# Last pass of a two-convolution residual block: the loads from the fourth input on move from SyncE's queue to ScalarE's

## What is computed

```python
def block(x, w1, b1, gamma1, beta1, w2, b2, gamma2, beta2):
    identity = x
    out = conv3x3(x, quantize_weight(w1, 8), b1)
    out = relu(batchnorm(out, gamma1, beta1))      # statistics over all images
    out = conv3x3(out, quantize_weight(w2, 8), b2)
    out = batchnorm(out, gamma2, beta2)            # statistics over all images
    return relu(out + identity)

return x + block(_gn(x), w1, b1, gamma1, beta1, w2, b2, gamma2, beta2)
```

## Time and profile before

| | |
|---|---|
| timed runs (3), median | 525.36 us (524.45 to 526.71) |
| profiled execution, its own time | 525.32 us |
| span of the profiled execution | 523.5 us |
| PE busy in the span | 489.3 us (93%) |
| DVE busy | 453.3 us (87%) |
| ScalarE (ACT) busy | 367.6 us (70%) |
| DMA queue 1 (SyncE's): share of the 16 engines | 45.9% of the span |
| DMA queue 10 (ScalarE's): share | 0.2% |

### The profile page before, as it was taken

The page is one execution under the profiler, slowest core; times in us unless marked ns, Lnnn a source line. Parts: engine busy times, 40 slices in busy tenths (PEclk is TensorE's granted clock), DMA queues, the critical chain, the costliest instruction groups (busy, mean ns, idle before and its releaser), DMA issues.

```text
span 523.5 us, 23701 instructions
## 1 busy us (share of the span) xinstructions
PE 489.3 (93%) x10987; PEld 401.3 (77%) x10987; DVE 453.3 (87%) x648; ACT 367.6 (70%) x408; POOL 86.8 (17%) x155
## 2 busy tenths in 40 slices
PE   4999999999999999999999999999998898978982
PEld 2888777778999787899888889889887466557541
DVE  7999989999999966998887898878796989998894
ACT  4799899999899964766656555566631899686471
POOL 2027356666651200000000000000001000000000
PEclk9999999999999999999999999999998999989997
DMA  8934785543333000001344300000047899999997
GB/s 289 351 131 132 256 274 171 193 134 134 131 136 130 9 10 7 3 4 62 129 173 152 128 3 4 3 4 4 3 160 270 327 387 416 424 397 422 396 427 320
DMA packets 23242, 92.99 MB, mean 178 GB/s; under 512 B 8168, under 2 KB 9576, under 8 KB 19048
## 3 DMA queue, kind: packets, MB, share of 16 engines
q1 hardware_dynamic: 22960, 91.19, 45.9%
q10 hardware_dynamic: 184, 0.30, 0.2%
HBM read 58.27 MB, written 32.28 MB: 173 GB/s over the span
## 4 chain that ended last, share of the span: by engine, by line
PE 85%; DVE 8%; issue 2%; ACT 2%; DMA 1%; DVEq 0%; SPq 0%; ACTq 0%
PE conv_ps L1423 71%; PE conv_ps L1568 5%; PE conv_ps L1591 4%; PE conv_ps L1545 2%; DVE slots L1318 2%; DVE slots L1296 2%; DVE slots L1302 2%; PE conv_ps L1386 1%; DMA slots<-in_x_dram 1%; PE conv_ps L1553 1%; DVE bn_tup L1105 1%; DVE split L1325 0%; ACT split L822 0%; ACT conv_ps L796 0%; DVE xa L1318 0%
## 5 line engine op out<-in xcount | busy, mean ns | idle before, releaser
L1423 PE MATMUL conv_ps<-split,wmat 64*64 64x385 f16 (+3 forms) x9216 | 380.3, 324 | 0.7 <-ACT split L627 0.7
L1423 PEld LDWEIGHTS conv_ps<-split,wmat 64*64 64x64 bf16 x9216 | 326.2, 107 | 50.9 <-issue 1.4
L661 ACT ACTIVATE slots<-conv_ps,par,evac_scale 128x784 f32<-128x784 f32 x124 | 123.7, 998 | 94.6 <-PE conv_ps L1423 92.8
L1105 DVE BATCH_NORM_STATS2 bn_tup<-slots 128x6 f32<-128x392 f32 x164 | 80.8, 555 | 12.8 <-ACT slots L661 12.8
L992 DVE BATCH_NORM_STATS2 small<-slots 128x6 f32<-128x448 f32 x112 | 61.7, 612 | 0.8 <-DMA slots<-in_x_dram 0.8
L1070 DVE TENSOR_TENSOR split<-slots,split 128x3136 f16<-128x3136 f32 (+4 forms) x36 | 57.2, 1607 | 3.6 <-ACT split L627 0.8
L1072 DVE SCALAR_TENSOR_TENSOR split<-slots,split 128x3248 f16<-128x3248 f32 (+3 forms) x18 | 53.6, 2979 | 2.3
L1048 DVE TENSOR_SCALAR slots<-slots,bn_w 128x3248 f32<-128x3248 f32 (+3 forms) x18 | 30.4, 1687 | 19.6 <-ACT split L617 19.1
L617 ACT ACTIVATE split<-slots,bn_w 128x3248 f16<-128x3248 f32 x14 | 43.1, 3082 | 0.0
L669 ACT ACTIVATE xa<-conv_ps,par,evac_scale 128x784 bf16<-128x784 f32 x40 | 39.8, 997 | 0.0
L617 ACT ACTIVATE split<-slots,gn_b_all,gn_s_all 128x3136 f16<-128x3136 f32 x12 | 35.9, 2993 | 0.0
(11 more groups left out here) (159 smaller groups left out, 414.9 us busy)
## 6 DMA issues: line engine op xcount, KB each, us to landing
slots<-in_x_dram SPq DMA_DIRECT2D x13, 1568.0 KB, 11.5
slots<-in_x_dram SPq DMA_DIRECT2D x51, 392.0 KB, 5.2
out_dram<-slots SPq DMA_DIRECT2D x12, 784.0 KB, 8.4
out_dram<-slots SPq DMA_DIRECT2D x6, 1568.0 KB, 7.7
y_spill<-slots SPq DMA_DIRECT2D x3, 1624.0 KB, 6.2
slots<-y_spill SPq DMA_DIRECT2D x3, 1624.0 KB, 7.3
xa<-in_x_dram SPq DMA_DIRECT2D x2, 1568.0 KB, 11.0
split<-in_x_dram SPq DMA_DIRECT2D x2, 1568.0 KB, 10.2
```

The lines of the kernel that those rows point to most:

```text
L661: nc.scalar.activation(dst, src, ACT.Identity, bias=bias, scale=scale, accum_out=total).then_inc(evacuated[ph], 1)
L1105: ins = nc.vector.bn_stats(bn_tup[:, 2 * (n - first) + s, :], rows[s])
L1423: return nc.tensor.matmul(bank[:, r0:r1, w0:w1], lhs, rows[:, top + r0:top + r1, w0 + kx - 1:w1 + kx - 1], start=n == 0 and part is hi_all ...
```

## The change

All loads from input 4 on, and the reload of kept sums for input 15, are taken off SyncE's list and put into ScalarE's, each with its wait, at a chosen place. Their order among themselves is the same. The stores stay on SyncE's list in the same order, and so do the loads of inputs 7, 0, 1, 2 and 3 and the first part of input 4's. Nothing that is computed changes. The core of the diff:

```diff
@@ SyncE's list @@
             store_first()
             store_ring(1)
-            wait_stored(0)
-            load(4)
             store_ring(2)
             store_ring(3)
-            wait_out(3)
-            load(5)
-            wait_stored(2)
-            load(6)
             store_half(4, 0)
-            wait_stored(3)
-            load(8)
             store_half(4, 1)
-            wait_out(4)
-            load(11)
             store_half(5, 0)
             store_half(5, 1)
-            wait_out(5)
-            load(9)
-            wait_stored(4)
-            load(10)
             store_whole(6)
-            load(12)
             store_whole(7)
-            reload_sums(0)
             store_half(8, 0)
             store_half(8, 1)
-            load(14)
-            wait_stored(7)
-            load(13)
             store_half(9, 0)
             store_half(9, 1)
-            load(15)
             store_whole(10)
@@ new on ScalarE @@
+            def load(u):
+                first = EARLY if u == IN_STRIPS else 0
+                sc.dma_start(x3[u][:, first:], pair_view(x, PAIR3[u])[:, first:]).then_inc(x3_loaded[u], 16)
+
+            def load_over_stored(u, before):
+                sc.wait_ge(stored[before], 16 * STORES[before])
+                load(u)
+
+            def load_over_input(u, before):
+                if before in TWO_PASS:
+                    sc.wait_ge(two_out, first_two(before) + 2)
+                else:
+                    sc.wait_ge(ring_out, nth(before, NQ - 1))
+                load(u)
+
+            def reload_sums(n):
+                u = NP - KEPT + n
+                sc.wait_ge(stored[RELOADED[u]], 16 * STORES[RELOADED[u]])
+                sc.wait_ge(y2_spilled[n], 16)
+                sc.dma_start(slot3(u)[:, 0:PIX], y2_spill[n]).then_inc(y2_loaded[n], 16)
@@ ScalarE's list @@
-            for u in (2, 3):
-                for k in range(NQ):
-                    seed(u, k)
-            for n in range(2):
-                make_act1(0, n)
-                make_hi1(0, n)
+            for k in range(NQ):
+                seed(2, k)
+            load_over_stored(4, 0)
+            for k in range(NQ):
+                seed(3, k)
+            make_act1(0, 0)
+            make_hi1(0, 0)
+            make_act1(0, 1)
+            load_over_input(5, 3)
+            make_hi1(0, 1)
+            load_over_stored(6, 2)
             two_affine(4, 0)
             two_affine(4, 1)
             make_act2(0, 0)
             two_affine(5, 0)
+            load_over_stored(8, 3)
             make_act2(0, 1)
             two_affine(5, 1)
             make_act2(0, 2)
+            load_over_input(11, 4)
             two_affine(6, 0)
             make_act2(0, 3)
             two_affine(6, 1)
             seed_again(0, 0)
             seed_again(0, 1)
             two_affine(8, 0)
+            load_over_input(9, 5)
+            load_over_stored(10, 4)
             seed_again(0, 2)
             two_affine(8, 1)
             seed_again(0, 3)
-            for n in range(2):
-                make_act1(1, n)
-                make_hi1(1, n)
+            make_act1(1, 0)
+            make_hi1(1, 0)
+            load_over_input(12, 6)
+            make_act1(1, 1)
+            make_hi1(1, 1)
+            reload_sums(0)
             two_affine(9, 0)
             make_act2(1, 0)
             two_affine(9, 1)
             make_act2(1, 1)
             two_affine(10, 0)
             make_act2(1, 2)
+            load_over_input(14, 8)
             two_affine(10, 1)
+            load_over_stored(13, 7)
             make_act2(1, 3)
-            for q in range(NQ):
-                seed_again(1, q)
+            seed_again(1, 0)
+            seed_again(1, 1)
+            load_over_input(15, 9)
+            seed_again(1, 2)
+            seed_again(1, 3)
```

More of the change, by code:

```diff
@@ L415, in load @@
             def load(u):
-                first = EARLY if u == IN_STRIPS else 0
-                sp.dma_start(x3[u][:, first:], pair_view(x, PAIR3[u])[:, first:]).then_inc(x3_loaded[u], 16)
+                sp.dma_start(x3[u], pair_view(x, PAIR3[u])).then_inc(x3_loaded[u], 16)
             def wait_stored(u):
@@ L454, in store_whole @@
                 sp.dma_start(pair_view(out, PAIR3[u]), out_of(u)).then_inc(stored[u], 16)
[L456 to L460, removed]
             def store_ring(u):
```

## The result

| | before | changed |
|---|---|---|
| median of 20 timed runs | 525.53 us | 528.83 us |
| lowest and highest | 524.45 to 527.41 | 525.15 to 532.37 |
| ratio to before, 95% interval | | 1.006 (1.0045 to 1.0076) |
| profiled execution, its time and span | 525.32, 523.5 us | 525.59, 523.8 us |

The forecast was 529.3. The changed kernel's times cover 7.2 us where the kernel before covers 3.0, and the execution that was profiled lies near the lowest. A second profile of the same code (the first experiment) caught one of 530.19 us. The two together show more than either.

What follows compares the result with a forecast made beforehand. The prediction took the compute chain through PE as the bound. Load 8 holding ScalarE 5.0 us, less 1.07 us of slack, made add_parts about 4.0 us late, with issues at 0: 525.3 + 4.0 = 529.3 us, 8-in-10 range 525.0 to 530.9.

Steps and rivals of the forecast that it cites:

- Bound: Last pass: the compute chain through PE sets the end, not the DMA engines; only one 0.5 us compute wait on transfers.
- Issue time on ScalarE: Loads 5, 6, 8 and 11 on busy ScalarE: 0.6 to 1.1 us if serial; taken as 0, 1.1 kept for the range.
- Load 8's wait, 5.0 us: Before make_act2(0, 1), ScalarE waits for input 3's stores until 440.4 instead of going on at 435.44; PE 3.9 us late.
- the sign that I had set: Idle before make_act2(0, 1) under 1.5 us and store landing before 437 would mean a wrong queue share, time 525 to 526.
- my share of the queues: Input 3's stores beside loads 5 and 6: turns packet by packet give the stores one third, landing at 440.4.
- Sum: The end of the kernel moves as much as PE's add_parts, 4.0 us: 525.3 + 4.0 = 529.3.
- Eleven waits are over by today's times: Eleven of ScalarE's twelve added waits are for events already over when it arrives; load 6 tight at 0.2 us.
- Load 6's hold: ScalarE's wait for both stores of input 2, landing at 429.0, after make_hi1(0, 1) ends at 428.82: 0.2 us.
- The last store's 7.0 us stay: At the kernel's end, the last store still takes 7.0 us to land, since all loads are over by then.
- the stores keep their share: Rival: input 3 lands at 436.6, load 8 holds ScalarE 1.2 us, 525.4, no change; chance 0.28.
- Serial issues as the main cost: Rival: ScalarE pays for each issue, 4 x 0.55 less 1.07 is 1.1 us, stores in time: 526.4; chance 0.12.
- A gain in bandwidth from two queues: Prediction saw no bandwidth to win at DMA share 1.01; its faster rival, better interleaving, gained 0.5 us: 524.8; chance 0.08.

Runs made afterwards that it cites:

- run 1: The changed kernel itself timed again, 12 runs, nothing edited: median 526.52 us, 1.0025 of the kernel before; its profile is of a 530.19 us execution.
- run 6: run 3's kernel with load 8 alone back at the change's place, ahead of the second make_act2: 527.69 us, 1.0048 of the kernel before.
- run 3: The changed kernel with loads 4, 8, 10 and 13 moved later on ScalarE, all twelve transfers still issued there: 524.89 us, 0.9991 of the kernel before.
- run 10: run 3's kernel timed again on a second chip: 525.24 us, 1.0007 of the kernel before.
- run 7: run 3's kernel with load 13 alone back at the change's place, ahead of input 11's last make_act2: 524.91 us, 0.9994 of the kernel before.
- run 4: The kernel before with only loads 5 and 6 moved to ScalarE, at the change's places: 525.84 us, 1.0019 of the kernel before.
- run 2: The changed kernel with load 8 alone moved later, behind input 7's last make_act2: 526.50 us, 1.0025 of the kernel before.
- run 5: run 3's kernel with load 4 alone back at the change's place, ahead of input 3's seeds: 525.92 us, 1.0016 of the kernel before.
- run 8: The changed kernel with loads 5 and 6 each issued as two halves: 526.24 us, 1.0024 of the kernel before.
- run 9: The kernel before, loads still on SyncE, with the five store waits alone added to ScalarE at the change's places: 525.69 us, 1.0009.

## Why the prediction was right, and where it was not

- **Bound.** Right for the holds: what stops ScalarE for 4 us at load 8 comes out at the end (runs 1 and 6), and runs 3 and 10, with all loads on the second queue and input 3's store as late as in the change, cost nothing. Not right for the last microseconds, where the transfers count too (see the last store below).
- **Issue time on ScalarE: taken as 0.** Right where an activation is running: the issue at 425.70 is hidden, and run 3 has all twelve issues at 0.9991. Where a wait has emptied ScalarE first, the issue comes on top of it, 0.38 us at load 6 (431.44 to 431.82) and 0.43 to 0.44 at loads 8 and 13. The prediction kept the issues of loads 8 and 11 for the range only; load 8's belonged in the sum.
- **Load 8's wait, 5.0 us.** The place and the mechanism were right, shown by run 1's profile (3.98 us, 2.13 us of it seen by PE at add_parts) and by run 6, which brings back 0.48% with this line alone. The size is that of the long executions: I gave one number where the chip gives 0.96 to 4.0. Input 3's store landed 8.6 and 10.8 us after input 2's where I had 11.4, and 13.6 us after it in run 6's profile. By the sign that I had set (idle time under 1.5 us, a landing before 437) the first profile says that my share of the queues was wrong; the packet counts say that it was right, 2 to 1 in bytes. What failed is the step from the share to the landing. It doesn't depend simply on how much of the stores is left when load 5 comes: load 5 was issued 2.1 us before input 2's store landed in the first profile, 3.7 us before it in run 1's and 0.6 us after it in run 6's, and input 3's store took 10.7, 14.5 and 13.0 us from issue to landing; run 7's, with load 5 0.3 us after, took 9.2.

  The late landings are a matter of a few rows. In run 4's trace (store issued at 425.97, landed at 440.2) all rows of input 3's stores but six have started by 435.2; the six start at 435.68, 436.38, 437.08, 437.78, 438.48 and 439.19, 0.70 us apart. A row of the store takes 0.24 us there and a row of a load 0.47, together 0.71: just what one DMA engine would show that is behind the others and takes one row of each queue in turn. In run 1's trace the last rows start in pairs at such distances, up to 441.08, while most had started by 436. So the share was as forecast and the landing is that of the slowest of the 16 engines (this reading rests on the times; the records don't name the engine). Why one or two of them are behind in some executions is open.
- **Sum.** +4.0 forecast, +3.3 as the difference of the medians. That the two are so near is partly luck. In the profiles the hold was 4.0 at most and not 5.0, and 1.4 us are given back at the end, which the sum has not; on the other side stand the holds at load 6 and ahead of make_hi1, and the issue behind each wait. No profile is of an execution near the median of 528.83. And the same code was slower by only 1.4 us in run 1.
- **Eleven waits are over by today's times.** This step failed. The wait of make_hi1 for input 1's stores was in the kernel before and I left it out of the list: it is on the way to PE's first convolution, and load 4, now beside those stores, makes the second take 8.7 us in place of 5.8 (rows of the changed kernel and of the one before):

```profile
out_dram<-split SPq DMA_DIRECT2D x1, 784.0 KB, 8.7
```

```profile
out_dram<-split SPq DMA_DIRECT2D x1, 784.0 KB, 5.8
```

  It held ScalarE by 0.5 to 1.1 us in every profile with load 4 at the change's place. Load 6's hold, priced at 0.2 us, was 0.9 in run 1 and 1.3 in run 4. Load 13's wait was not over either: input 7's store landed at 480.5 in the first profile, at 477.0 before. Its hold costs nothing that run 7's times show.
- **The last store's 7.0 us stay.** Wrong. The later the last store is issued, the less it takes to land (us; profiles with this store in one piece; runs 2, 4, 5, 6, 7 and 8, not shown, fit in to 0.3 us):

| profile | issued | us to land | landed |
|---|---|---|---|
| run 3 | 514.07 | 7.6 | 521.65 |
| before | 516.02 | 7.0 | 523.04 |
| run 10 | 517.44 | 5.8 | 523.22 |
| change | 517.72 | 5.6 | 523.30 |
| run 9 | 517.94 | 5.6 | 523.51 |
| run 1 | 522.37 | 5.6 | 527.92 |

  In the kernel before the store still queues behind others (DMA share 1.02 from 512 to 520 us, against 0.90 in the first profile of the change). So the first 1.7 us by which the compute chain comes late cost only 0.3 us at the end; that is why the execution of the first profile, with three holds, took 525.59 us. Run 9, with no hold and one queue, shows the same 5.6, so this is no property of the two queues.
- **Rivals.** That the stores keep their share fell with the packet counts. They are better ground than the stretch at the kernel's start that I used: 44 against 34 packets are not equal turns. Serial issues as the main cost fell with run 3. A gain in bandwidth from two queues is not there.

The rule of the Trainium skill that was weighed (page DMA: Bandwidth & Descriptors, section Queues, rings and completion order: turns between queues, packet by packet) agrees with the four counts above in so far as both queues get equal numbers of rows. It has packets of several descriptors; the last rows of run 4's store speak for one row a turn, and the measurement decides here.

**Still open.** Run 1 found 1.0025 for the code that 20 runs before had put at 1.006, and run 6 found more (1.0048) with one hold than run 1 with all; the intervals of the first two don't overlap. How often an execution falls into the long hold may differ from chip to chip; no run tests it. Why run 2, without load 8's hold, was no quicker than run 1 is settled in part at most: its profile has load 13's hold on the chain, but run 7's times show no cost of that hold. Single profiles can't size a hold of a microsecond: from the first store of `out` to the issue of the last one 108.9, 110.8, 112.1 and 113.3 us pass in run 3, the kernel before, run 10 and run 9, none of which has a hold by a store. The change has 112.9 in its first profile; only run 1 (115.6) and run 6 (117.6) lie clearly above. The sizes of the single holds are therefore known only roughly: load 8 about 0.5% on its chip, load 4 about 0.15% and not certain, load 13 nothing that was measured.

## What to carry to other kernels

When a load moves to another queue, ask what it was standing behind: in one queue the store issued first was served first, in two both got equal numbers of rows, so the transfer with the longer rows got the larger share. A wait that was over "by the times of before" isn't over any more if what it waits for now shares the engines; put it behind work that can't start earlier than the worst landing, or leave it on an engine that has nothing to compute. And time such a change in many runs: one profile of this kernel showed a loss of 0.3 us, another 4.9, of which 1.5 came from the earlier passes, which the change leaves alone.

## What the hardware did that I had not expected

- The same code took from 525.15 to 532.37 us in 20 runs, while the kernel before stayed within 3.0 us (within 4.0 to 4.2 in the sets of 35). Load 8's wait by itself gives such a spread (run 6, 8.0 us), since the store that it waits for landed 9.2 to 14.5 us after its issue in the ten profiles with loads 5 and 6 whole on the second queue. A late landing is that of its last few rows, 0.70 us apart in run 4's trace; what puts them behind is open.
- ScalarE's queue issues a transfer while an activation is running, 0.33 to 0.37 us each, with no gap behind it. When ScalarE has run empty in a wait ahead of the issue, the next activation starts 0.38 to 0.44 us after the issue begins.
- A store of 1568 KB at the end of the kernel took 7.6 us to land when it was issued at 514 us and 5.6 from 517.7 on: while the DMA engines are behind, lateness of the compute chain is largely given back.
